# A four-layer graph network on one core: first edge stage, two of sixteen destination tiles fetched by GpSimd, the cast of the weighted rows on ScalarE

## The reference, cut to what matters

```python
Wh = h @ W + b
Wr, Wc = Wh[row], Wh[col]                    # row = src, col = dst
sim = sum(Wr * Wc) / max(|Wr| * |Wc|, 1e-8)
base = adj_v * softplus(deg_coeff[0] * deg_v + deg_coeff[1]) * (row != col)
prop_pos = segment_sum((base * relu(sim))[:, None] * Wc, row)
prop_neg = segment_sum((base * -relu(-sim))[:, None] * Wc, row)
x = x + scale * (c0 * prop_pos + c1 * prop_neg + c2 * Wh)
```

## Time and profile before

| | |
|---|---|
| median of 3 runs | 6714.87 us (6709.61 to 6737.81) |
| profiled execution, its own time | 6677.32 us |
| its span | 6675.1 us |
| granted TensorE clock, mean | 0.829 |
| PE busy / DVE / ACT / POOL | 70% / 62% / 28% / 47% |
| the changed stage | about 85 to 2115 us of the span |

### The profile page before, as it was taken

One profiled execution on the slowest core, in us unless ns is written; L12 is line 12 of the kernel. 1 busy time (PEld: TensorE's weight loads), 2 busy tenths in 40 slices (PEclk: granted clock), 3 DMA queues, 4 the chain that ended last, 5 costly groups with the idle time before them and its releaser, 6 DMA issues. The chain is left out here.

```text
span 6675.1 us, 100965 instructions
## 1 busy us (share of the span) xinstructions
PE 4704.2 (70%) x28624; PEld 3007.3 (45%) x28624; DVE 4170.2 (62%) x7653; ACT 1888.7 (28%) x6318; POOL 3155.2 (47%) x2946
## 2 busy tenths in 40 slices
PE   3777777777777676667566666663777777739998
PEld 2333333333334333333344554452444444418997
DVE  4454444444446666666666666664666766688997
ACT  1333333333333000000133333331000000016775
POOL 3433343333331655555354454452666666515554
PEclk7778787888888788888677878886999888869999
DMA  3222222222221111111111111111443334411111
GB/s 84 55 54 51 53 56 52 52 51 54 55 54 32 38 38 38 39 39 36 26 41 38 41 40 38 41 40 32 108 111 108 110 110 117 110 49 51 49 49 34
DMA packets 492408, 379.08 MB, mean 57 GB/s; under 512 B 345930, under 2 KB 378971, under 8 KB 492339
## 3 DMA queue, kind: packets, MB, share of 16 engines
q1 hardware_dynamic: 394803, 288.65, 15.3%
q0 software_dynamic: 90560, 83.37, 7.0%
q10 hardware_dynamic: 6976, 6.23, 0.3%
HBM read 341.76 MB, written 36.12 MB: 57 GB/s over the span
## 5 line engine op out<-in xcount | busy, mean ns | idle before, releaser
L1009 POOL DMA_INDIRECT edge_src_rows<-table_wh,edge_gather_idx x806 | 787.1, 977 | 1169.5 <-DVE edge_small L1128 924.6
L1038 PE MATMUL edge_sums_ps<-edge_onehot_src,edge_halves 128*128 128x512 bf16 x4840 | 1048.3, 361 | 302.5 <-issue 296.5
L892 POOL DMA_INDIRECT edge3a_src_rows<-table_h,edge3a_gather_idx x808 | 764.3, 946 | 564.1 <-issue 311.2
L2040 PE MATMUL edge3a_z_ps<-Wz,edge3a_both_ends_t 128*128 128x396 f32 x1616 | 695.3, 579 | 365.2 <-DVE edge3a_terms L2133 315.1
L1114 DVE TENSOR_SCALAR edge_onehot_src<-layer_node_row,edge_src_col,edge_magnitude 128x1568 bf16<-128x1568 f16 x605 | 410.5, 679 | 842.8 <-remote 471.6
L892 POOL DMA_INDIRECT table_cat<-table_hn,table_gather_idx x592 | 599.5, 1013 | 631.6 <-PE edge_cat_t_ps L1720 340.4
L1401 POOL DMA_INDIRECT edge_src_rows<-table_h,edge_gather_idx x608 | 606.9, 998 | 553.9 <-PE edge_msg_ps L1433 190.8
L1038 PEld LDWEIGHTS edge_sums_ps<-edge_onehot_src,edge_halves 128*128 128x128 f16 x4840 | 428.0, 104 | 872.7 <-issue 537.7
L2133 DVE SCALAR_TENSOR_TENSOR edge3a_terms<-edge3a_z_ps,att_z 128x792 f32<-128x792 f32 x404 | 386.0, 977 | 406.1 <-DMA edge_edge_attr<-in_ea 223.9
L2040 PEld LDWEIGHTS edge3a_z_ps<-Wz,edge3a_both_ends_t 128*128 128x128 f32 x1616 | 333.5, 217 | 670.1 <-DVE edge3a_terms L2133 359.6
L2452 PE MATMUL edge3b_sums_ps<-edge3b_onehot,edge3b_weighted 128*128 128x128 f32 x4848 | 572.7, 278 | 6.2 <-DVE layers_accT L2490 4.5
(11 more groups left out here) (372 smaller groups left out, 8320.9 us busy)
## 6 DMA issues: line engine op xcount, KB each, us to landing
edge_dst_row<-in_dst_row SPq DMA_DIRECT2D x102, 512.0 KB
edge3a_dst_row<-in_dst_row SPq DMA_DIRECT2D x102, 512.0 KB
edge_window<-table_wh SPq DMA_DIRECT2D x816, 32.5 KB
edge3a_window<-table_h SPq DMA_DIRECT2D x816, 32.0 KB
edge_edge_attr<-in_ea SPq DMA_DIRECT2D x101, 256.0 KB
kept_rows<-edge3a_src_rows SPq DMA_DIRECT2D x101, 256.0 KB
edge3b_src_rows<-kept_rows SPq DMA_DIRECT2D x101, 256.0 KB
edge_edge_attr<-in_ea SPq DMA_DIRECT2D x101, 128.0 KB
```

What stands on the lines that cost most here:

```text
L892: nc.gpsimd.indirect_dma_start(self.slot(b, j), None, self.table[:, :], bass.IndirectOffsetOnAxis(ap=self.idx[b][:, j:j + 1], axis=0)).the ...
L1009: nc.gpsimd.indirect_dma_start(g[q][:, j, :], None, k.t_wh[:, :], bass.IndirectOffsetOnAxis(ap=idx[q][:, j:j + 1], axis=0)).then_inc(gathe ...
L1038: mm = pe.matmul(acc[:, i, 0:w], halves[q][:, j, a, :, :].rearrange("p h d -> p (h d)"), hot[:, o:o + w], start=first and a == 0, stop=False)
L2040: mm = pe.matmul(zp[q % 2][:, i, 0:H * ZH], hcT[h][:, j * P:(j + 1) * P], k.Wz[:, :], start=True, stop=True)
```

## The change

Four things are edited, all in `edge0`:

1. The destination rows of the last two tiles of each pair (14 and 15) come no longer from a window and a product on PE. SP loads 14 windows, PE's parts become 5, 5 and 4 tiles, and POOL fetches the two tiles' rows by index, right into `dst_rows`, after the 16 gathers of the source rows. For these two it waits for `v_done` of the pair two before, since `weighted` reads the buffer that they fill. SP loads their two columns of indices in a transfer of its own.
2. The fp16 cast (`high`) goes from DVE to ACT. On ACT it stands after the one-hot of tile 11 and ahead of the copy of the third part.
3. `low` goes on DVE from the end of a pair's body to the next body, behind the one-hots of tiles 0 and 1 and ahead of `products`.
4. `products` waits for 18 gathers in place of 16, and `weighted` waits for the `low` of the pair before.

```diff
-    PARTS = ((0, 6), (6, 11), (11, PB))
+    BY_PE = PB - 2
+    PARTS = ((0, 5), (5, 10), (10, BY_PE))
...
+        own = [c.sb(f"dst_idx{q}", [P, PB - BY_PE], I32) for q in (0, 1)]
...
-                    wait_past(sp, gathered[q], 16 * PB * m)
+                    wait_past(sp, gathered[q], 16 * (2 * PB - BY_PE) * m)
+                    sp.dma_start(own[q][:, :], k.dst_t[:, bass.ds(t * PB + BY_PE, PB - BY_PE)]).then_inc(idx_loaded[q], 16)
                     sp.dma_start(idx[q][:, :], k.src_t[:, bass.ds(t * PB, PB)]).then_inc(idx_loaded[q], 16)
...
+                            if h * B + j >= BY_PE:
+                                continue
                             sp.dma_start(win[q][:, h * B + j, :], k.t_wh[bass.ds(base, P), :]
                                          ).then_inc(win_loaded[q], 16)
...
-                    pool.wait_ge(idx_loaded[q], 16 * (m + 1))
+                    pool.wait_ge(idx_loaded[q], 32 * (m + 1))
...
+                    wait_past(pool, v_done, t - 1)
+
+                    pool.sem_inc(gate, 1)
+                    for j in range(BY_PE, tiles_of(t)):
+                        nc.gpsimd.indirect_dma_start(
+                            wcs[q][:, j, :], None, k.t_wh[:, :],
+                            bass.IndirectOffsetOnAxis(ap=own[q][:, j - BY_PE:j - BY_PE + 1], axis=0)
+                            ).then_inc(gathered[q], 16)
...
-                    pe.wait_ge(win_loaded[q], 16 * PB * (m + 1))
+                    pe.wait_ge(win_loaded[q], 16 * BY_PE * (m + 1))
...
+                def high(t, q):
+                    act.wait_ge(v_done, t + 1)
+                    wait_past(act, used_v, NV * (t - 1))
+                    wait_past(act, used_a, NA * (t - 1))
+                    act.activation(halves[q][:, :, 0, :, :], v[:, :, :, :], ACT.Copy).then_inc(hi_ready, 1)
...
+                high(0, 0)
                 one(0, 0, 0)
...
+                        if a == 2 and more(t, 1):
+                            high(t + 1, 1 - q)
...
-                    dve.wait_ge(gathered[q], 16 * (PB * m + tiles_of(t)))
+                    dve.wait_ge(gathered[q], 16 * ((2 * PB - BY_PE) * m + tiles_of(t) + max(0, tiles_of(t) - BY_PE)))
...
                 def weighted(t, q):
                     dve.wait_ge(split_done, t + 1)
+                    wait_past(dve, lo_ready, t)
...
                     one(t, q, 1)
+                    if not (isinstance(t, int) and t == 0):
+                        low(t, q)
                     if more(t, 1):
                         products(n, o, m + q)
...
                         weighted(n, o)
-                        high(n, o)
-                        low(n, o)
```

More of the change, by code:

```diff
@@ L1227, in _ @@
                 weighted(0, 0)
-                high(0, 0)
                 low(0, 0)
@@ L2507, in build @@
     k.scores_d = dram("scores_by_head", (H, BATCHES, B, P))
+    k.dst_t = ins["dst_t"]
     k.src_run = ins["src_run"]
```

5 lines of the change are left out of this document (removed).

## The result

The changed kernel takes 6746.53 us (median of 17 runs, 6740.79 to 6772.28) against 6714.43 us for the kernel before (17 runs, 6698.11 to 6753.05): 1.0046 times as long, 95% interval 1.0032 to 1.006, so 32 us slower where I forecast 20 us less. The profiled execution took 6740.79 us, its span is 6739.0.

The account below looks back on a forecast made before the run. No engine was full; some 15 us of a pair's 40 were put down to PE's trickle during POOL's gathers and what follows it. Terms -23 - 5 + 8 = -20 us took the median from 6714.87 to 6695 us, range 6635 to 6765.

Parts of the forecast that it names:

- the -23 us for PE's four products: First stage's pairs: four fewer PE products save 0.46 us a pair over 51 pairs; bounds nothing to twice that.
- the clock's -5: PE's clock returning to full level at another time after the earlier end of work: -5 us, bounds +15 and -35.
- two more gathers, cost 0: POOL's two late gathers each pair neither delay the next run nor starve PE: 0, at worst 4.2 us a pair.
- rival 2: The two gathers starve PE just after `v_done`: 6888 us, or 6791 if the store is half filled; chance 0.12.
- The forecast of 39.6 to 39.9 us: Sign in the changed kernel's profile: the time of a pair in the first stage's steady part.
- The stop: PE's near-idle stretch once a pair, called the trickle; forecast still some 12.5 us, ending about 2 us after sixteen gathers.
- rival 4: ACT's cast holds up the third copy, up to 2.0 us a pair: 6787 us, or 6741 at 1 us; chance 0.11.
- Rival 1: PE's clock comes back sooner in each pair and the gain doubles or more: about 6656 us; chance 0.25.
- Rival 3: Window loads cause PE's trickle, so two fewer shorten it by 2.7 us: 6589 us; chance 0.07.
- The opening: Start of the first stage: 36 gathers in place of 32 and the cast on ACT, +8 us, bounds 0 and +12.
- has time to spare: POOL in the first stage: it stands 914.9 of 1847 us waiting for DVE, so it can take more gathers.
- The store of instructions: PE works off about 120 stored instructions, not refilled while POOL gathers, then nearly stops once in each pair.

Follow-up runs that it names:

- no_late_gathers: Kernel before with PE selecting fourteen tiles and the other two tiles' rows fixed at 1.0, cast still on DVE: 5223.46 us, ratio 0.9986, without stops.
- pool_shift: Kernel before with twelve idle gathers once, behind the last gather of the first stage: 6755.94 us against 6732.48, ratio 1.0019, with stops.
- more_traffic: Kernel before with four more transfers a pair, about 2.1 MB, into tiles no one reads: 6659.93 us, ratio 0.9989, with stops.
- after_fourth: The changed kernel itself, measured again in a set with stops: 6763.61 us against 6727.61, ratio 1.0052.
- idle_gathers: Kernel before with two more gathers a pair that no one uses, PE still selecting sixteen tiles: 5337.56 us, ratio 1.02, without stops.
- four_gathers: Changed kernel with four destination tiles gathered a pair in place of two, PE selecting twelve: 5422.22 us, ratio 1.0358 to before, without stops.
- after_again: The changed kernel itself, measured again in a set without stops: 5283.99 us, ratio 1.0101 to before.
- one_gather: Changed kernel with one destination tile gathered a pair in place of two, PE selecting fifteen: 5225.28 us, ratio 0.9991 to before, without stops.
- cast_alone: Kernel before with only the cast moved to ACT and the subtraction later, sixteen tiles selected and sixteen gathers: 5230.44 us, ratio 0.9996, without stops.
- same_again: The kernel before, unchanged, profiled again in a set without stops: 5232.71 us, ratio 1.0004.

## Why the prediction was wrong, step by step

- **The first step that failed: the -23 us for PE's four products, and the clock's -5 with it.** cast_no_late, the change without its two gathers, is 0.14% faster than before in its set, 9 us (between 20 faster and 1 slower) where these terms say 28. Without stops no_late_gathers gives 7 us for the same products. The argument had been that all of the 0.46 us counts as it is saved where PE works without a wait. Work saved in a stretch that a stop ends anyway needn't come out at the end, and the lower bound of the term, "nothing", was the nearer one. That remark on the stop is argued, not shown.
- **The second step that failed: "two more gathers, cost 0".** The changed kernel differs from cast_no_late by them (and by the wait in front of them, and by POOL's longer program). It is 0.46 and 0.52% above before in its two sets (0.32 to 0.6 and 0.28 to 0.77), where cast_no_late is between 0.3% below and 0.02% above. So the two gathers cost about 0.6%, some 40 us by the ratios, though the sets are different ones. How they cost it stays open. It is not rival 2: PE doesn't starve beside them. The pair is 39.31 and 39.50 us against 38.88 in cast_no_late, but pool_shift has 39.36 with the old pair, so the profiles don't place the cost in the pair. Up to 25 us of it (13 by the ratio of pool_shift) may come from twelve more gathers ahead of the later stages alone.
- **The pair.** The forecast of 39.6 to 39.9 us was for the steady part, where before has 40.15. The 39.14 above is a mean that holds the last three pairs too, of 24 to 25 us each. From the third `weighted` to the 47th, 44 pairs, before has 40.17 us, more_traffic 39.77 and pool_shift 39.96, all with the old pair; the changed kernel has 39.91 and 40.28, and cast_no_late 39.62. So the first profile of the changed kernel fell nearly on the forecast, by luck: unchanged pairs scatter by 0.4 us from one profile to the next.
- **What held.** The stop is as long as before (PE nearly idle from 607.4 to 620.1), the late gathers stand 8 us behind the run and starve no one, and the cast takes 1.9 us and fits (rival 4 falls). Rival 1 falls: the granted clock of the steady part is 0.81 as in the earlier trace rows, and no gain came. Rival 3 falls: fourteen windows in place of sixteen shorten no stop.
- **The opening.** Forecast +8 us, with the first sums at about 147 us. They came at 163.4 once and at 144.3 the other time, each time 5.4 us after the start of the first cast on ACT (158.08 and 138.96), which stands there behind six copies that wait for PE. In the first profile PE stood 15.9 us without a releaser before the last of these parts, in the second it did not. The loss is not lasting: the last `weighted` is at 2094.3 and 2103.8, the one with the late opening first.
- **The stages behind.** The sum had no term for them, and the profiles put most of their difference there: 60 us between the first two, 71 us (1189.1 - 1118.0) by the two idle times between after_fourth and the profile of before. By medians within a set the whole change is 32 and 36 us. The profile of before is that of an unusually fast execution, and I could not get a second one with stops. So neither the sign nor the size of a part of the later stages is shown.
- **What the trace of one kind can't show.** In sets without stops the same change costs 1.0% through the same step that I had put at 0: two more gathers. The prediction argued that POOL "has time to spare", which is true only while stops make the pair 39 us long. With a pair of 25.2 us sixteen gathers fill POOL, and from the eighteenth on each one lengthens the pair by 1.2 to 1.3 us. Here the cause is shown, by idle_gathers and four_gathers.
- **The store of instructions.** The prediction's picture (POOL's gathers keep PE's store from being filled) describes the stops but is not their whole cause, since the same gathers denser still make none in the other sets. The profile of before also lists only 7 packets of instructions, 0.10 MB, between 200 and 2000 us (the two rows below, of its transfers view for this stretch), a time of 46 pairs. So no refill per pair is on record, and nothing here shows a store that empties. What decides between the two kinds of sets stays open; the chip alone does not, for chip 3 ran one set of either kind (after_again without stops, cast_no_late with them).

```profile
q8 instruction: 5, 0.08, 0.0%
q14 instruction: 2, 0.02, 0.0%
```

No variant beats the kernel before beyond doubt. Nearest are one_gather (0.9991) and cast_alone (0.9996) without stops; both were not run with them.

## What to carry to other kernels

Before giving an engine more work because it "has time to spare", ask how long its cycle would be if today's stall were gone, and add its work against that cycle: POOL had 20 us idle of 40 and none of 25. A small gain on an engine that is stopped by something else may be worth nothing, so leave the new work out once and time the saving alone. Before blaming a change for longer stages that it doesn't touch, compare a stretch that it can't have reached as well, and take both profiles from one set. And once GpSimd is the bound, count how long VectorE's wide operations hold its gathers, by where they begin, and not the cast alone.

## What the runs showed of the hardware that was not expected

- One program has two times, 5230 us and 6660 to 6730 us, set by set. The difference is in every stage with gathers: POOL's idle time in the third stage's edges is 328.9 us in one kind (same_again) and 564.1 in the other (before), for the same 808 gathers.
- A gather of 0.95 us that begins during a wide two-input VectorE operation (128 x 2048, fp32) ends 0.82 us after it and takes 1.9 to 2.9 us, with no cast near. With a cast to fp16 right behind, it takes 2.45 us and ends 0.11 us after the cast.
- Doubling the core's traffic (53 to 107 GB/s) changes neither the stops nor the time (0.9989).
